# A gated linear-attention layer with experts on one core: four inner products computed as unsplit float32 matmuls

## The reference

```
q = rope(xn @ Wq.T); k = rope(xn @ Wk.T); v = xn @ Wv.T      # k, v shared by 4 heads
dt = softplus(xn @ Win.T + dt_bias);  G = cumsum(dt * A) in each chunk
xc = v * dt
scores  = q_i . k_j                                  # per chunk
y_intra = (scores * causal exp(G_i - G_j)) @ xc
cstates = (k * exp(Glast - G))^T @ xc                # per chunk
state   = state * exp(Glast) + cstates               # carried from chunk to chunk
y_inter = (q * exp(G)) @ state_before
y = rmsnorm(y_intra + y_inter) * gnorm_w * silu(xn @ Wg.T);  out = y @ Wo.T
```

## Time and profile before

| | us |
|---|---|
| median of 3 runs | 2235.84 (2227.21 to 2246.15) |
| the profiled execution's own time | 2215.74 |
| its span, first to last instruction | 2213.9 |
| TensorE busy | 2046.6 (92%) |
| VectorE busy | 1882.1 (85%) |
| ScalarE busy | 1258.9 (57%) |
| GpSimd busy | 1054.9 (48%) |

### The profile page before, as it was taken

One profiled execution on the slowest core, in us unless ns is written; L12 is line 12 of the kernel. 1 busy time (PEld: TensorE's weight loads), 2 busy tenths in 40 slices (PEclk: granted clock), 3 DMA queues, 4 the chain that ended last, 5 costly groups with the idle time before them and its releaser, 6 DMA issues.

```text
span 2213.9 us, 34454 instructions
## 1 busy us (share of the span) xinstructions
PE 2046.6 (92%) x9824; PEld 1598.1 (72%) x9824; DVE 1882.1 (85%) x3440; ACT 1258.9 (57%) x2603; POOL 1054.9 (48%) x833
## 2 busy tenths in 40 slices
PE   5799999999999999999899999999999999989992
PEld 3677777777777777776677777777777777767772
DVE  5899899888888999868988888888888988837886
ACT  5565555555565555543555655555656565637882
POOL 2354445445454545444355555545555454534661
PEclk9899999999999999999999999999999999999996
DMA  6312121212121212135121212121212121128668
GB/s 250 91 51 56 45 57 47 57 47 57 40 64 35 67 36 67 37 91 176 38 67 39 63 38 62 38 67 38 67 38 67 36 66 32 53 95 273 215 213 318
DMA packets 147549, 182.33 MB, mean 82 GB/s; under 512 B 12936, under 2 KB 89320, under 8 KB 147455
## 3 DMA queue, kind: packets, MB, share of 16 engines
q1 hardware_dynamic: 137310, 155.52, 23.8%
q0 software_dynamic: 8704, 25.21, 3.2%
q10 hardware_dynamic: 1440, 0.58, 0.1%
HBM read 152.90 MB, written 28.37 MB: 82 GB/s over the span
## 4 chain that ended last, share of the span: by engine, by line
PE 83%; DVE 5%; issue 5%; DMA 3%; ACT 2%; POOL 1%; ACTq 0%; SPq 0%; DVEq 0%; POOLq 0%
PE PJ L1248 13%; PE PJ L1249 12%; PE PJ L1250 12%; PE OU L1248 5%; PE OU L1250 5%; PE OU L1249 5%; PE YE L1250 2%; PE YE L1249 2%; PE YE L1248 2%; PE SC L1248 2%; PE YI L1248 2%; PE CS L1248 2%; PE CS L1250 2%; PE CS L1249 2%; PE OU L1344 2%
## 5 line engine op out<-in xcount | busy, mean ns | idle before, releaser
L458 POOL TENSOR_TENSOR zl<-yb,zh 128x512 fp32r<-128x512 f32 x122 | 167.8, 1375 | 216.3 <-ACT zh L976 216.3
L1248 PE MATMUL PJ<-xnh,wqh 128*128 128x512 f32 x544 | 222.6, 409 | 14.2 <-DVE t L1795 14.2
L742 POOL TENSOR_TENSOR gm<-gbc,amask 128x512 f32<-128x512 f32 x128 | 167.3, 1307 | 139.1 <-DVE wfl L1881 90.5
L992 ACT ACTIVATE qh<-t 128x512 fp32r<-128x512 f32 x128 | 80.9, 632 | 252.9 <-DVE t L1798 252.9
L1248 PE MATMUL PJ<-xnh,wgh 128*128 128x512 f32 x512 | 211.4, 413 | 4.2 <-POOL wgl L712 4.2
L1249 PE MATMUL PJ<-xnl,wqh 128*128 128x512 f32 x544 | 214.1, 394 | 0.0
L1250 PE MATMUL PJ<-xnh,wql 128*128 128x512 f32 x544 | 214.0, 393 | 0.0
L1249 PE MATMUL PJ<-xnl,wgh 128*128 128x512 f32 x512 | 206.3, 403 | 0.0
L1250 PE MATMUL PJ<-xnh,wgl 128*128 128x512 f32 x512 | 205.6, 402 | 0.0
L1248 PE MATMUL OU<-woh,zh 128*128 128x512 f32 x488 | 191.4, 392 | 3.8 <-POOL zl L458 3.8
L1250 PE MATMUL OU<-woh,zl 128*128 128x512 f32 x488 | 191.0, 391 | 0.0
(11 more groups left out here) (557 smaller groups left out, 6238.3 us busy)
## 6 DMA issues: line engine op xcount, KB each, us to landing
gbc<-decay_exponents SPq DMA_DIRECT2D x128, 256.0 KB, 4.8
stage<-in_wq SPq DMA_DIRECT2D x72, 256.0 KB, 3.7
stage<-in_wg SPq DMA_DIRECT2D x64, 256.0 KB, 2.6
stage<-in_wo SPq DMA_DIRECT2D x64, 256.0 KB, 2.5
gbc<-in_wm SPq DMA_DIRECT2D x48, 256.0 KB, 3.1
stage<-in_wkv SPq DMA_DIRECT2D x34, 256.0 KB, 2.6
experts<-in_wm SPq DMA_DIRECT2D x16, 512.0 KB, 6.5
experts<-expert_rows SPq DMA_DIRECT2D x16, 512.0 KB, 13.3
```

What stands on the lines that cost most here:

```text
L458: nc.gpsimd.tensor_tensor(lo[:], yb[:, c, :], hi[:].bitcast(F32), ALU.subtract).then_inc(S["zlo"], 1)
L742: g.tensor_tensor(gm[:, c % 2, :].rearrange("p (h i) -> p h i", h=HG), gbc[:, c % 2, :].rearrange("p (h i) -> p h i", h=HG), amask[:].unsq ...
L1248: nc.tensor.matmul(out_, a_hi, b_hi, start=first, stop=False)
```

## The change

Keys, queries, values by rows, keys by rows, weighted values, weighted scores and states are no longer split; scores, chunk states, `intra` and `inter` are each one float32 matmul in place of three fp32r matmuls. Weights, normalised rows and gated outputs stay split. The copies to the high parts and the subtractions for the low parts go, with their semaphores; `rope` writes its result straight into the query tile (or, for the keys, into one half of `t2`); the three chunk states have a tile each. The mask on GpSimd now waits for the matmul that read the previous contents of `gm` (`yintra`) and not for the low part (`wlo`). In the first step VectorE, and not ScalarE, waits for the copies of the turned rows. Two of ScalarE's weight copies are placed otherwise around `z_hi(0)`.

```diff
+        kf, qf, vwf, knf = t2[:, 0, :], qhf, vwhf, as_f32("knh")
+        states = [st, sthf, stlf]
...
@@ gpsimd @@
                         if c < 2:
-                            at.before("wlo", c + 3)
+                            at.before("yintra", c + 3)
                         else:
-                            at.wait("wlo", c - 1)
+                            at.wait("yintra", c - 1)
...
-                    def rope_lo(i, hi, lo):
-                    def v_lo():
...
                         weight_lo(0)
                         weight_lo(1)
                         gmasked(0)
-                        rope_lo(0, kh[:], kl[:])
-                        v_lo()
-                        for j in range(4):
...
+                        weight_lo(2)
+                        if not first:
+                            z_lo(pool, at, 0)
+                        weight_lo(3)
+                        gmasked(1)
@@ scalar @@
-                            rope_hi(0, kh[:])
-                            v_hi()
-                            rope_hi(1, qh[:, 0, :])
+                            value_rows()
+                            weight_hi(2)
                             if not first:
                                 z_hi(at, 0)
-                            weight_hi(2)
+                            weight_hi(3)
                             at.wait("coef", 1)
-                            vw_hi(0)
-                            kn_hi()
-                            weight_hi(3)
-                            rope_hi(2, qh[:, 1, :])
+                            weighted(0)
+                            key_rows()
                             decay(0)
-                            rope_hi(3, qh[:, 2, :])
-                            rope_hi(4, qh[:, 3, :])
                             if not first:
                                 z_hi(at, 1)
                             silu_gate(0)
                         for c in range(NCH):
-                            at.wait("wsc", c + 1)
-                            if c:
-                                at.wait("yintra", c)
-                            a.activation(wfh[:], gm[:, c % 2, :], ACT.Copy).then_inc(S["whi"], 1)
...
-                                a.activation(sth[:], st[:], ACT.Copy).then_inc(S["sthi"], 1)
@@ tensor @@
-                            mm3(SC[:].rearrange("p (h i) -> p h i", h=HG), kh[:, cs], kl[:, cs], qh[:, :, cs],
-                                ql[:, :, cs], True, True).then_inc(S["score"], 1)
+                            nc.tensor.matmul(SC[:].rearrange("p (h i) -> p h i", h=HG), kf[:, cs], qf[:, :, cs],
+                                             start=True, stop=True).then_inc(S["score"], 1)
...
-                            mm3(CS[:], knh[:, c, :], knl[:, c, :], vwh[:], vwl[:], True, True).then_inc(S["cstate"], 1)
+                            nc.tensor.matmul(CS[:], knf[:, c, :], vwf[:], start=True, stop=True).then_inc(S["cstate"], 1)
...
                         def inter(c):
-                            at.wait("stlo", c)
+                            at.wait("stt", c)
...
-                                ins = mm3(YE[:, hs], sth[:, hs], stl[:, hs], qh[:, h, cs], ql[:, h, cs], True, True)
+                                ins = nc.tensor.matmul(YE[:, hs], states[c - 1][:, hs], qf[:, h, cs], start=True,
+                                                       stop=True)
...
                         def intra(c):
-                            at.wait("wlo", c + 1)
+                            at.wait("wsc", c + 1)
+                            if c == 0 and first and half == 0:
+                                pe.wait_ge(gt_copied, 2)
...
-                            mm3(YI[:], vh[:, cs], vl[:, cs], wfh[:], wfl[:], True, True).then_inc(S["yintra"], 1)
+                            nc.tensor.matmul(YI[:], vf[:, cs], gm[:, c % 2, :], start=True, stop=True).then_inc(
+                                S["yintra"], 1)
...
-                        at.wait("ropelo", 4)
-                        at.wait("q3lo", 1)
+                        at.wait("rope", 5)
                         scores(0)
@@ vector @@
                         def rope(i, bank):
...
+                            turned = qf[:, i - 1, :] if i else kf
                             at.wait("proj", (1, 3, 4, 5, 6)[i])
                             if i == 0:
-                                at.before("ropelo", 4)
+                                at.before("score", 4)
                             elif i == 1:
-                                at.before("q3lo", 1)
-                            else:
-                                at.wait("ropelo", i - 1)
-                            if i == 2:
-                                at.wait("tr", 2)
+                                at.before("yinter", 3)
...
+                            for done in xts_out:
+                                dve.wait_ge(done, 32)
                             rope(1, 0)
...
-                        vw_lo(0)
-
-                        at.wait("ropehi", 5)
-                        v.tensor_tensor(ql[:, 3, :], t2[:, (5 * b + 4) % 2, :], qh[:, 3, :].bitcast(F32),
-                                        ALU.subtract).then_inc(S["q3lo"], 1)
-                        at.wait("knhi", 1)
-                        v.tensor_tensor(knl[:], TR[:, 0:3 * P].rearrange("p (a b) -> p a b", a=3),
-                                        knh[:].bitcast(F32), ALU.subtract).then_inc(S["knlo"], 1)
                         weigh(0)
                         gated(0)
                         for c in range(NCH):
-                            at.wait("whi", c + 1)
-                            v.tensor_tensor(wfl[:], gm[:, c % 2, :], wfh[:].bitcast(F32),
-                                            ALU.subtract).then_inc(S["wlo"], 1)
...
-                                if c < 2:
-                                    vw_lo(c + 1)
...
-                                v.tensor_tensor(stl[:], st[:], sth[:].bitcast(F32), ALU.subtract).then_inc(
-                                    S["stlo"], 1)
```

More of the change, by code:

```diff
@@ L297, in build @@
             proj=10, tr=2, score=4, cstate=3, yinter=3, yintra=4, ssq=1, spread=1, oproj=4,
-            vraw=1, ropehi=5, vhi=1, knhi=1, dec=4, expg=3, vwhi=3, whi=4, sthi=3, tanh=4, ysq=4,
+            vraw=1, vt=1, kn=1, dec=4, expg=3, vw=3, tanh=4, ysq=4,
             rsln=1, rms=1, zhi=4,
-            coef=1, roperd=5, rope=5, q3lo=1, knlo=1, wsc=4, wlo=4, vwlo=3, stt=3, stlo=3, yt=3, y=4, gated=4, u=4, z=4, accd=4,
-            ropelo=4, vlo=1, gmask=4, zlo=4,
+            coef=1, roperd=5, rope=5, wsc=4, stt=3, yt=3, y=4, gated=4, u=4, z=4, accd=4,
+            gmask=4, zlo=4,
         )
@@ L988, in head @@
                             return hcoef[:, b, kind, c, h:h + 1]
-                        def rope_hi(i, hi):
-                            at.wait("rope", i + 1)
-                            a.activation(hi, t2[:, (5 * b + i) % 2, :], ACT.Copy).then_inc(S["ropehi"], 1)
                         def decay(c):
@@ L1808, in weigh @@
                             ins.then_inc(S["wsc"], 1)
-                        def vw_lo(c):
-                            at.wait("vwhi", c + 1)
-                            for h in range(HG):
-                                hs = slice(h * P, (h + 1) * P)
-                                ins = v.scalar_tensor_tensor(vwl[:, hs], vf[:, c * P:(c + 1) * P], head(2, c, h),
-                                                             vwh[:, hs].bitcast(F32), ALU.mult, ALU.subtract)
-                            ins.then_inc(S["vwlo"], 1)
                         def head_coefs():
@@ L1897, in step @@
                                 if c == 0:
+                                    at.before("yinter", 3)
                                     v.tensor_copy(st[:], CS[:]).then_inc(S["stt"], 1)
                                 else:
-                                    at.wait("sthi", c)
                                     at.wait("stt", c)
@@ L1903, in step @@
                                         hs = slice(h * P, (h + 1) * P)
[L1904 to L1905 removed]
+                                        ins = v.scalar_tensor_tensor(states[c][:, hs], states[c - 1][:, hs],
+                                                                     head(3, c, h), CS[:, hs], ALU.mult, ALU.add)
                                     ins.then_inc(S["stt"], 1)
```

83 lines of the change are left out of this document (21 added, 62 removed).

## The result

The changed kernel takes 2141.42 us (median of 4 runs, 2136.75 to 2156.85), the kernel before 2233.31 us beside it (4 runs, 2227.21 to 2246.15). The profiled execution of the changed kernel is the slowest of its runs, 2156.85 us with a span of 2155.1.

The account below looks back on a forecast made before the run. TensorE's column time plus its standstills, chiefly 54.4 us before the scores, was taken as the bound. Products +21, wait -59, last `intra` -4 and clock -8 gave -50 us: 2235.84 to 2186, range 2160 to 2230.

Parts of the forecast that it names:

- Part 4: Work taken off VectorE, ScalarE and GpSimd: only the last `intra` of a step gains, 4 us; rotation waits mostly stay.
- Part 6: Half-speed clock stretches right behind the wait at the scores: five expected gone, -8 us, bounds 0 and -8.
- Parts 1 and 2: Eleven 512-column calls at 0.86 us, +1.93 us a step; twelve 128-column `inter` products, 0.87 a chunk, -1.26 a step.
- rival 1: The eleven 512-column float32 products cost more, 1.07 us each: 2261 us, or 2287 by passes; chance together 0.06.
- Part 3: TensorE's wait before a step's first scores goes, -59 us; lateness of `rope(4)`'s add at most 0.2 us a step, should be nothing.
- Part 5: New waits, such as GpSimd's mask 1.8 us later: covered, so nothing added; first step 0 to 4 us once, taken as 0.
- Rivals 2 to 4: `inter` gains nothing, 2226, 0.08; half the wait returns elsewhere, 2217, 0.08; clock falls more often, 2240, 0.07.
- The 20 us between profile and median: The kernel before's median, 2235.84, lay 20 us above its profiled execution; the forecast subtracted 50 from that median.
- Rival 5: More is won: other half-speed stretches, part of the 14.2 us and the 20 us go, -15 to -25 more, 2166; chance 0.10.

Follow-up runs that it names:

- the first pair of experiments: The kernel before and the changed kernel, each measured once more with no edit: 2229.33 us and 2146.38 us.
- the second pair: The same repeat of the kernel before and the changed kernel without edits: 2229.33 us and 2146.38 us.
- b_again: The kernel before, measured once more with no edit: median 2229.33 us, ratio 1.000.
- a_again: The changed kernel, measured once more with no edit: median 2146.38 us, ratio 0.963 to the kernel before.
- the changed kernel with load: The changed kernel with VectorE's 21 removed instructions a step put back, unread: 2152.18 us; with its second loop moved by 110 instructions, which brought the fetches, 2157.69 us.
- the one with split states: The changed kernel with the chunk states of chunks 1 and 2 split again: 2169.84 us, ratio 0.971 to the kernel before.

## Why the prediction was right in direction and too small

The step that failed most is Part 4. It had the 14.2 us of waits for a rotation stay and VectorE's lost work off the chain; the profiles show 14 us of instruction fetches gone and 12 us won on the way from half to half. Part 6 was a smaller miss, 13 us of stretches against 8.

- **Parts 1 and 2**, the prices of the products, hold: 0.86 us a 512-column call, and eight instructions of `inter` take 0.81 (the 747.89 start to the next projection at 748.70), against 0.87 forecast. The other price, that of rival 1, is out. The Trainium skill's "4 passes" ("FP8 and Floating Point Precision", "TensorE Precision Notes") agrees as a count of streams, 0.86 = 4 x 0.215, but the split's three cost 0.228 each, and so the factor between them is 1.26 here and not 4/3; at 128 columns it is 0.20 against 0.32, the other way.
- **Part 3** holds in its size. The wait is gone, the scores come 0.14 behind, for the add of `rope(4)`, within the 0.2 allowed. Put back alone, 1.7 us a step returns. Its reason for "nothing" was misread. The add that took 1.15 at 704.91 did not run beside a rotation's subtraction, but beside the mask, which doesn't go away:

```profile
704.22 1.30 POOL L742 TENSOR_TENSOR gm<-gbc,amask 128x512 f32<-128x512 f32 x1
```

In the changed kernel `z_lo` runs there, and the add takes 1.53. One of 0.69 would have ended at 736.98, before TensorE was through with its last gate matmul. To move `z_lo` wasn't tried.

- **Part 5** holds: no wait in a step took the place of the old one. **Rivals 2 to 4** didn't happen, and no step of the loops lost clock to the float32 streams.
- **The ordinary step** is therefore right: -1.44 measured, -1.4 forecast, 45 us over the 31 steps.
- **Part 4 failed in one sentence**, "the 14.2 us mostly stay too". The margin of 0.14 does stay: keys' rotation off the bank at 718.43 + 0.68 = 719.11, query projection at 719.25. But the 14.2 us in 9 were not cut from that margin. Most were the loop's instruction fetches, seen as `hcoef` waiting on "issue": without the fetches 4.3 us in 3 are left. I put down a wait of TensorE to VectorE and never asked what VectorE had waited for. In the profile of the kernel before from the first pair of experiments six steps of the second half are longer by 1.4 to 3.1 us besides their clock, 14 us in all, and none in the changed kernel.
- **Part 4 failed in another**, "None of it stood on the chain outside part 3": where the second half begins, VectorE has routing to do as well. There the change won 12 us beyond the ordinary step, and putting VectorE's instructions back costs 9 of them.
- **Part 6 was too small.** It counted five stretches in one execution, at 8 us, and made that its bound. That execution had six of them among these steps, and was the shortest of all on record; the one of the second pair had eight, 8 x 1.6 = 13 us.
- **The 20 us between profile and median** were carried over to the changed kernel whole. They are for the most part time at half speed, but whether the change takes any of it away is open, as said above. The miss is nearly as large without them: 38 us from profiled to profiled execution, 42 from median to median.

The account is over the profiled executions of `b_again` and `a_again`, 2226.59 to 2138.42, 88 us where 50 were forecast. From the first to the last `spread_scales`, 1823.3 to 1739.4: ordinary steps 45, stretches 13, fetches 14, the way from half to half 12, together the 84 us between them. The other 4 of the 88 lie ahead of and behind the layers' steps. So of the 38 us that the forecast lacks, 26 are Part 4's, 5 Part 6's, 3 the ordinary step's and 4 lie outside. The shares are read from windows; the experiments bear out the wait and the 9 of the 12. The fetches are less sure: taking them from the kernel before won 9 us net, since more steps fell to half speed. Rival 5 named the mechanism (stretches and part of the 14.2 us) and gave 2166; it had 0.10 and was also too small.

How the fetches end is partly luck: by the count above a body of up to 257 instructions can't lie across a fourth packet, and the change made it 242, but the kernel before would have lost them as well by 25 instructions of padding. What stays open is why the fetches in the changed kernel with load cost nothing, while they cost 2.6 us a pass and more in the one with split states; that in each the packet moves at another point of the step is a guess, and wasn't tried.

## What to carry to other kernels

Where the timed runs lie above the profiled execution and their clock below, the difference is time at half speed: look in several profiles where it can lie before you carry it over or count it as won. Follow a wait to its end: when the engine waited for stood on "issue" itself, count the packets of the instruction queue in the loop, and move the loop by a few idle instructions before explaining anything else; it costs one run. Splitting is a choice for each product: wide ones whose parts are ready in time are cheaper split, narrow ones and those on the last wait are cheaper unsplit.

## What was not expected of the hardware

- A loop of 260 to 286 instructions on VectorE is fetched anew in each pass or not at all, by its place: 25 packets of 8 KB in five passes, or none. It cost from nothing to 3.1 us a pass, and with the stretch that followed up to 4.7.
- Standing still for 1.55 to 1.63 us before the scores lowered TensorE's clock in no step of 29, 1.75 to 1.83 us in 2, 2.17 to 2.24 us in 23, to 0.50 and at some 1.7 us a time. With split products 1.72 to 1.77 us did so only in steps with another stall, 1.78 to 1.89 us in 24 of 56.
- A float32 add of 128x512 on VectorE takes 0.69 us with nothing on GpSimd beside it, and up to 1.59 beside a GpSimd subtraction.
- Two products of 512 columns: 0.86 us unsplit, 0.685 in three; of 128 columns: 0.20 unsplit (0.81 for four), 0.32 in three. So unsplit is dearer at 512 columns and cheaper at 128.
